# Loading an image by colour channel, another order of the last attention turn, and one transpose for half a group's maxima

## The reference

```python
# tokenizer: 8 images of 256 x 256 x 3, then 128 text rows of width 256 each
g = einsum('bhwc,cd->bhwd', x, ccm) + ccm_bias
g = sum(slopes * relu(g[..., None] - shifts), axis=-1)      # 16 points, slopes are 0 beyond the first
h = clip(einsum('bhwc,co->bhwo', g, conv_w) + conv_b, 0, 1)[..., 0]
h = concatenate([h, txt], axis=1)                           # 8 x 384 tokens of width 256
# causal attention, 16 heads of 16, keys and values through a latent of 64
c_kv = ln(h) @ W_DKV;  k = c_kv @ W_UK;  v = c_kv @ W_UV;  q = ln(h) @ W_UQ
h = h + softmax(causal(q @ k.T / 4)) @ v @ W_O
# 8 experts, the two best per token, 384 slots per expert and choice
scores = softmax(ln(h) @ router_w)
y_e = gelu(x_e @ w1[e]) @ w2[e]                             # 256 -> 1024 -> 256
h = h + sum over the two choices of y * weight + bias
```

## Time and profile before

| | |
|---|---|
| median of three runs | 658.73 us (657.36 to 666.75) |
| the profiled execution | 664.39 us, span 662.7 us |
| PE, PEld busy | 608.2 us (92%), 508.2 us |
| DVE, ACT, POOL busy | 399.6, 377.1, 388.4 us |
| share of the last chain | PE 80%, ACT 5%, issue 5%, DVE 3% |
| front half, expert half | about 0 to 366 us, 366 to 663 us |

### The profile page before, as it was taken

The page is one execution under the profiler, slowest core; times in us unless marked ns, Lnnn a source line. Parts: engine busy times, 40 slices in busy tenths (PEclk is TensorE's granted clock), DMA queues, the critical chain, the costliest instruction groups (busy, mean ns, idle before and its releaser), DMA issues.

```text
span 662.7 us, 13744 instructions
## 1 busy us (share of the span) xinstructions
PE 608.2 (92%) x5082; PEld 508.2 (77%) x5082; DVE 399.6 (60%) x950; ACT 377.1 (57%) x818; POOL 388.4 (59%) x602
## 2 busy tenths in 40 slices
PE   1788999999999999999878899999999999999992
PEld 1465666676767666666558899999999999999992
DVE  5789788788998888678464333334554555344320
ACT  4448786777777785765641554445454454545540
POOL 4303233424556555556556499998877777888223
PEclk9979999999999999999899799999999999999997
DMA  6437676633534232371012825454444434442113
GB/s 231 124 80 179 196 203 179 182 102 99 145 98 113 72 104 82 105 221 36 34 48 63 285 93 110 115 112 112 112 110 81 97 82 105 112 109 45 20 23 38
DMA packets 66604, 73.86 MB, mean 111 GB/s; under 512 B 6312, under 2 KB 61586, under 8 KB 66536
## 3 DMA queue, kind: packets, MB, share of 16 engines
q1 hardware_dynamic: 56232, 59.45, 30.3%
q0 software_dynamic: 9504, 13.00, 11.5%
q10 hardware_dynamic: 800, 0.52, 0.3%
HBM read 31.62 MB, written 22.48 MB: 82 GB/s over the span
## 4 chain that ended last, share of the span: by engine, by line
PE 80%; ACT 5%; issue 5%; DVE 3%; DMA 2%; SPq 1%; POOL 1%; ACTq 0%; DVEq 0%; POOLq 0%
PE t_bank L1790 20%; PE bank L1805 14%; PE s_bank L1805 7%; PE bank L695 7%; PE t_bank L660 5%; PE s_bank L638 5%; PE t_bank L754 3%; PE s_bank L639 2%; PE t_bank L723 2%; PE s_bank L1775 1%; PE t_bank L738 1%; PE t_bank L760 1%; PE bank L707 1%; DVE g L1235 1%; ACT part L1032 1%
## 5 line engine op out<-in xcount | busy, mean ns | idle before, releaser
L1752 DVE TENSOR_TENSOR hl<-h,hh 128x384 fp32r<-128x384 f32 x128 | 102.9, 809 | 157.9 <-ACT h L1715 157.9
L553 POOL TENSOR_SCALAR_AFFINE_SELECT pt<-pt 128x256 f32<-128x256 f32 x192 | 82.0, 433 | 150.2 <-ACT pt L973 116.7
L1192 DVE TENSOR_REDUCE mx<-s_bank 128x2 f32<-128x256 f32 (+2 forms) x192 | 122.9, 683 | 34.2 <-PE s_bank L639 33.7
L1712 ACT ACTIVATE hh<-t_bank 128x384 fp32r<-128x384 f32 x128 | 63.0, 492 | 135.0 <-PE t_bank L1790 132.7
L1665 POOL DMA_INDIRECT out<-yo,xr x48 | 74.8, 1558 | 59.1 <-ACT yo L1723 48.9
L973 ACT ACTIVATE pt<-t_bank 128x512 f32<-128x512 f32 x128 | 76.1, 602 | 30.6 <-PE t_bank L660 29.4
L1652 POOL TENSOR_TENSOR wl<-wr,wh 128x256 fp32r<-128x256 f32 x112 | 92.5, 859 | 1.2
L1790 PE MATMUL t_bank<-xh,wh 128*128 128x384 f32 x256 | 87.1, 340 | 0.6 <-DVE xl L1746 0.6
L1790 PE MATMUL t_bank<-xl,wh 128*128 128x384 f32 x256 | 86.5, 338 | 0.0
L1790 PE MATMUL t_bank<-xh,wl 128*128 128x384 f32 x256 | 86.4, 338 | 0.0
L638 PE MATMUL s_bank<-ks,qs 96*128 96x128 bf16 (+2 forms) x384 | 80.0, 278 | 1.6 <-DMA ks<-part 1.5
(11 more groups left out here) (205 smaller groups left out, 1341.4 us busy)
## 6 DMA issues: line engine op xcount, KB each, us to landing
wr<-in_w SPq DMA_DIRECT2D x16, 1024.0 KB, 5.8
qs<-part SPq DMA_DIRECT2D x96, 96.0 KB
ks<-part SPq DMA_DIRECT2D x90, 96.0 KB
slot_rows<-empty SPq DMA_DIRECT2D x4, 1560.0 KB, 9.4
xr<-slot_rows SPq DMA_DIRECT2D x16, 390.0 KB, 3.3
wr<-in_x SPq DMA_DIRECT2D x8, 768.0 KB, 5.5
out<-hid SPq DMA_DIRECT2D x8, 384.0 KB, 6.2
qs<-mT ACTq DMA_DIRECT2D x64, 3.0 KB
```

The source lines that it names most:

```text
L553: pool.affine_select(out=blocks, in_=blocks, compare_op=ALU.is_ge, fill=0.0, base=0, pattern=[[0, 2], [1, P]], channel_multiplier=-1).then ...
L1192: ins = dve.tensor_reduce(mx[:, p // 2, j, 2 * (p % 2):2 * (p % 2) + 2], pair_region(s_bank, j), AX_X, ALU.max)
L1752: dve.tensor_tensor(hl[:, f, :], h[f % 2][:, :], hh[:, f, :].bitcast(F32), ALU.subtract).then_inc(hl_done, 1)
```

## The change

Seven groups of edits are made together.

- Image 0 comes in three transfers, one for each colour channel, with a semaphore each; ACT waits for the first alone, DVE for the second and the third.
- On POOL the clearing of `empty`, the `token` table and the ones of `vb` move behind the first root; the split of `up` leaves POOL: its high part goes to ACT, its low part to DVE, between the variances and the scaling of entry 0. The statistics of entry 0's text rows move on DVE ahead of its colours.
- The maxima are kept heads before tiles, so one transpose of 128 x 24 takes the place of three of 128 x 8; ACT copies 24 x 128 in place of 8 x 384, and each of the two rows goes out from 12 partitions of 256 bytes in place of 4 of 768. In the last turn SP issues these two transfers for heads 4 to 7, not ACT.
- The last turn is reordered: PE ranks entry 5 earlier, projects entry 6 later and transposes entry 6's rows after projecting entry 7; ACT copies turn 14's contexts after the last exponentials; DVE makes entry 5's slots first, splits the first expert's first matrix itself (copy and subtraction, two halves) between its attention work, and POOL sends entry 5's rows between its clips.
- PE's fillers become full-precision (f32) ones: `turned` (128 columns each) in seven places and `spinning` (11 of 512 columns) in place of the last 200.
- The bias of the last entries moves on DVE into the first expert unit, and SP loads the second expert's weights ahead of the stores.
- POOL's one subtraction of 2048 columns becomes eight of 256.

```diff
-        load_x(0)
+        wide = IT * W
+        for c in range(CH):
+            sp.dma_start(xin[0][:, c, :, :].rearrange("p j w -> p (j w)"),
+                         x[0][:, c * wide:(c + 1) * wide]).then_inc(x_first[c] if c < CH - 1 else x_in[0], 16)
...
-        pool.memset(empty[:, :, :], 0.0).then_inc(empty_made, 1)
...
-        pool.wait_ge(mats_in, 16)
-        pool.tensor_copy(up_h[:, :], up).then_inc(up_split, 1)
-        pool.wait_ge(up_split, 1)
-        pool.tensor_tensor(up_l[:, :], up, up_h[:, :].bitcast(F32), ALU.subtract).then_inc(up_split, 1)
         rstds(0)
+        pool.wait_ge(xn_done, NT)
+        pool.memset(empty[:, :, :], 0.0).then_inc(empty_made, 1)
...
         for p in range(4):
             for unit in range(3):
                 clip(END, p, unit)
+            if p:
+                send(B - 3, p - 1)
         rstds2(B - 2)
-        for i in range(TOPK * NT):
-            send(B - 3, i)
+        send(B - 3, 3)
+        pool.wait_ge(cx_sb, NG * END + 2)
+        send(B - 3, 4)
         rstds2(B - 1)
+        send(B - 3, 5)
...
-            for j in range(NT):
-                mm = pe.transpose(M_b[0:MPARTS * GH, j * P:(j + 1) * P],
-                                  ms[:, grp, j, :, :].rearrange("p a h -> p (a h)"), ident_b[:, :])
-            mm.then_inc(mT_ps, 1)
+            pe.transpose(M_b[0:MPARTS * GH * NT, 0:P], ms[:, grp, :, :, :].rearrange("p a h j -> p (a h j)"),
+                         ident_b[:, :]).then_inc(mT_ps, 1)
...
+        def turned(count):
+
+            for _ in range(count):
+                pe.matmul(t_bank[:, 1, 0:P], ident[:, :], ident[:, :], start=True, stop=True)
+
+        def spinning(count):
+
+            pe.wait_ge(empty_made, 3)
+            flat = empty.rearrange("p k d -> p (k d)")
+            for _ in range(count):
+                pe.matmul(t_bank[:, 1, :], ident[:, :], flat[:, 0:512], start=True, stop=True)
...
-            act.activation(mT[:, grp, :], M_b[0:MPARTS * GH, 0:T], ACT.Copy).then_inc(mT_sb, 1)
+            act.activation(mT[:, grp, :], M_b[0:MPARTS * GH * NT, 0:P], ACT.Copy).then_inc(mT_sb, 1)
...
+        text_norms(0)
         for i in range(6):
             colours(0, i)
...
+        dve.wait_ge(up_split, 1)
+        dve.tensor_tensor(up_l[:, :], up, up_h[:, :].bitcast(F32), ALU.subtract).then_inc(up_split, 1)
         scaled(0)
...
-        early_low(dve)
-        for b in range(LATE, B):
-            late_bias(b)
...
-        stores(sp)
         for i in range(2):
             load_weights(1, i)
+        stores(sp)
...
+    def early_first(dve, half):
+
+        cols = slice(half * NW // 2, (half + 1) * NW // 2)
+        dve.wait_ge(w_in[0], 16)
+        dve.tensor_copy(wh[0][0][:, cols], wr[0][:, cols]).then_inc(w_first[0], 1)
+        dve.wait_ge(w_first[0], half + 1)
+        dve.tensor_tensor(wl[0][0][:, cols], wr[0][:, cols], wh[0][0][:, cols].bitcast(F32),
+                          ALU.subtract).then_inc(w_split[0], 1)
```

More of the change, by code:

```diff
@@ L139, in _ @@
         def _(dve):
-            before.vector(dve, behind.early_low)
-            behind.vector(dve)
+            before.vector(dve, behind.early_first)
+            behind.vector(dve, before.biases)
 def front(nc, common, lent, wr, w_in, routed, x, txt, params, mats, w1, w2, slot_rows, out):
@@ L273, in front @@
     x_in = [sem(f"x_in{q}") for q in range(2)]
+    x_first = [sem(f"x_first{c}") for c in range(CH - 1)]
     empty_made = sem("empty_made")
@@ L412, in store, with max_rows @@
                      hid[:, b, :, :]).then_inc(res_out, 16)
+    def max_rows(queue, n, grp):
+        queue.wait_ge(mT_sb, NG * n + grp + 1)
+        for a in range(MPARTS):
+            queue.dma_start(qs[(n // 2) % 2][n % 2][MROW + a:MROW + a + 1, grp * GH:(grp + 1) * GH, :],
+                          mT[a * GH * NT:(a + 1) * GH * NT, grp, :]).then_inc(m_in[grp], 16)
     def stores(sp):
@@ L774, in rows_back @@
             if b == B - 2:
-                take("last" if c else "logits", rowT_sb, KC * b + c + 1)
+                take("ranks" if c else "logits", rowT_sb, KC * b + c + 1)
             else:
@@ L923, in tensor @@
         shifted_scores(END, 0, 2)
+        ranks(B - 3)
         shifted_scores(END, 1, 0)
@@ L928, in tensor @@
         contexts_back(END - 1, 1, False)
-        project(B - 2, 0)
-        ranks(B - 3)
         shifted_scores(END, 2, 0)
@@ L939, in tensor @@
         shifted_scores(END, 3, 1)
+        project(B - 2, 0)
         shifted_scores(END, 3, 2)
+        project(B - 2, 1)
         values(END, 1)
+        turned(2)
         contexts_back(END, 1, False)
+        turned(3)
+        contexts_out(END, 0)
+        turned(2)
+        for k in range(2):
+            project(B - 1, k)
         for c in range(KC):
             rows_back(B - 2, c)
-        contexts_out(END, 0)
-        for k in range(2):
-            project(B - 1, k)
+        turned(3)
         router(B - 2)
-        turning(30)
+        turned(7)
         for c in range(KC):
@@ L1056, in scalar @@
         act.activation(uq, uq, ACT.Copy, scale=float(SCALE)).then_inc(prepared, 1)
+        act.activation(up_h[:, :], up, ACT.Copy).then_inc(up_split, 1)
         for d in range(CH):
@@ L1177, in scalar, with late_bias, vector @@
         gates(B - 1)
-    def vector(dve, early_low):
+    def late_bias(dve, b):
+        dve.wait_ge(row_done, (NT + 1) * b + NT + 1)
+        dve.tensor_tensor(hid[:, b, :, :], hid[:, b, :, :],
+                          bias.rearrange("p (o d) -> p o d", o=1).to_broadcast([P, NT, DIM]),
+                          ALU.add).then_inc(res_last, 1)
+    def vector(dve, early_first):
         steps = [0]
@@ L1230, in colours @@
             c, d = 1 + i // CH, i % CH
+            if b == 0 and d == 0:
+                dve.wait_ge(x_first[1] if c == 1 else x_in[0], 16)
             if c == 1:
@@ L1492, in vector @@
         mark(B - 3)
+        weigh(B - 3)
+        keep_ranks(B - 3)
+        place(B - 3)
         reciprocals(END - 1, 1)
         normalise(END - 1, 1)
+        dve.wait_ge(t_ready, 12 * END)
+        early_first(dve, 0)
+        reciprocals(END, 0)
+        normalise(END, 0)
+        early_first(dve, 1)
         residual(B - 2, 0)
         norms2(B - 2, (0, 1))
-        weigh(B - 3)
-        reciprocals(END, 0)
-        normalise(END, 0)
         residual(B - 2, 1)
@@ L1502, in vector @@
         variances2(B - 2)
[L1503 to L1505 removed]
         reciprocals(END, 1)
         normalise(END, 1)
+        scaled2(B - 2)
         residual(B - 1, 0)
@@ L1686, in early_high @@
     def early_high(act):
-        for i in range(2):
-            act.wait_ge(w_in[i], 16)
-            for half in range(2):
-                cols = slice(half * NW // 2, (half + 1) * NW // 2)
-                act.activation(wh[i][0][:, cols], wr[i][:, cols], ACT.Copy).then_inc(w_first[i], 1)
-    def early_low(dve):
+        act.wait_ge(w_in[1], 16)
         for half in range(2):
             cols = slice(half * NW // 2, (half + 1) * NW // 2)
-            dve.wait_ge(w_first[0], half + 1)
-            dve.tensor_tensor(wl[0][0][:, cols], wr[0][:, cols], wh[0][0][:, cols].bitcast(F32),
-                              ALU.subtract).then_inc(w_split[0], 1)
+            act.activation(wh[1][0][:, cols], wr[1][:, cols], ACT.Copy).then_inc(w_first[1], 1)
+    def early_first(dve, half):
[5 more added lines that the diff above has]
+                          ALU.subtract).then_inc(w_split[0], 1)
     def scalar(act):
@@ L1763, in vector @@
                     hidden(u + 1, f)
+                if u == 0 and f in BIAS_AT:
+                    biases(dve, BIAS_AT.index(f))
                 if u + 2 < U and f == ROWS_AT:
```

85 lines of the change are left out of this document (40 added, 45 removed).

## The result

The changed kernel takes 655.5 us, the median of 20 runs (652.77 to 657.84), where the kernel before takes 659.79 us in 20 runs (657.09 to 666.75). The ratio is 0.9925, with an interval of [0.9903, 0.9948]: 5.0 us less, between 3.4 and 6.4 (the two medians alone lie 4.3 us apart). That is within 2%. It is 3.1 us short of the 8.1 us foreseen; the time itself lies 4.9 us above the forecast of 650.6 us and only 0.5 us inside the end of the range, 656.0 us. The profiled execution took 655.22 us with a span of 653.5 us, at its median; that of before lay 4.6 us above the median of its 20 runs.

What follows compares the result with a forecast made beforehand. PE was taken to bound the kernel, with gains only at the start, in its attention instructions and before the experts. 2.4 + 2.8 + 2.9 = 8.1 us off 658.73 gave 650.6 us, range 644.0 to 656.0.

Steps and rivals of the forecast that it cites:

- the maxima: Attention turns: two fewer PE transposes, 32 times, save 3.5 us of PE; taken as 2.8 us, between 0 and 3.5.
- the turn with the sends: Last turn to the experts' first rows: 1.0 us from reordering plus 1.9 from sends, 2.9 us, between 0.9 and 4.2.
- the clock at the experts' start is full: Experts' start: a listed sign that the prediction is wrong, since it expected the half-clock stretch there to stay.
- Start: Kernel start: earlier parameters and first channel 1.4 us, shorter colour instruction 1.0; 2.4 us, between 1.0 and 3.2.
- The long colour instruction: DVE at the start: the last colour instruction should take about 0.74 us instead of 1.76, winning 1.0 us.
- three transfers would land no earlier: Image load at the start: parameters land as before; 1.4 us less gain, 652.0 us, within a rival of chance 0.18.
- In the PE-bound middle this is time: Attention turns: step counting PE's saved transposes as run time, except where DVE ends the wait; four fifths taken, 2.8 us.
- The rival that I had priced, the rows landing late: Maxima transfers: 12 short pieces make PE wait each half group; 666.6 us at 0.5 us each; chance 0.05.
- The sends: POOL's three first-choice sends of entry 7: DVE's subtractions and bias no longer beside them; 1.9 us won.
- first rival: Last ranks and experts' start: the clock stays up, 2.2 us plus 1.4 us more gained, 647.0 us; chance 0.18.
- the 0.7 us given back: Last turn: entry 6's rows, f32 fillers and router 6's delays take 0.7 us from the 1.7 us won.
- I leave the clock as it was: Experts' start: PE's gap before the first rows stays over 3 us, so no clock gain was counted.

Runs made afterwards that it cites:

- e1: The kernel before with the start edits alone (image 0 by channel, POOL's and DVE's order, split of `up`): 663.34 us, ratio 0.9973 to the kernel before.
- e2: The kernel before with the maxima edits alone (one transpose per half group, short copy, 12-piece transfers): 667.32 us, ratio 1.0025 to the kernel before.
- e5: The whole change with the old maxima (three transposes, rows in 4 pieces of 768 bytes): 652.83 us, ratio 0.9893 to the kernel before.
- e7: The whole change with one transfer of 24 pieces per half group's maxima instead of two of 12: 653.57 us, ratio 0.9900 to the kernel before.
- e11: The change with the old maxima, but one transfer of 8 pieces of 768 bytes per half group: 652.53 us, ratio 0.9884 to the kernel before.
- e9: The whole change with 170 bf16 products of 128 columns replacing the last filler of 11 f32 products: 658.04 us, ratio 0.9948 to the kernel before.
- e10: The whole change with the three bias additions on DVE directly behind the last ranks again: 656.51 us, ratio 0.9942 to the kernel before.
- e12: The whole change run once more with no edit: 655.2 us, ratio 0.9921 to the kernel before.
- e4: The whole change with the old bf16 fillers in their old places: 667.21 us, ratio 1.0014 to the kernel before.
- e3: The whole change without its start and maxima parts: 657.64 us, ratio 0.9886 to the kernel before.
- e6: The kernel before with only its three fillers behind the last turn replaced by the new f32 ones: 660.73 us, ratio 1.0006 to the kernel before.
- e8: The change with the old maxima plus six f32 filler products on PE in turn 0: 652.66 us, ratio 0.9894 to the kernel before.

## Why the prediction was right in its range and 3.1 us off

The time came into the range by luck. One of the three terms of the sum, the maxima, had the wrong sign; another, the turn with the sends, was foreseen at less than half of what its part gives alone; and the clock at the experts' start is full, which the prediction itself had named as a sign that it is wrong.

**Start: right, somewhat small.** Foreseen 2.4 us. PE's first transposes come at 17.93 us and not 19.95, 2.0 us earlier; alone the part gives 1.8 us (e1). The long colour instruction went as foreseen. The parameters came 0.93 us earlier and not 1.4, and DVE waited 0.96 us for the text, whose statistics I had only moved. The Trainium skill ("DMA: Bandwidth & Descriptors", Rules for kernel authors) wants many small transfers made into one, and the prediction read from it that three transfers would land no earlier. The pieces here are 256 KB, and the trace shows a gain. (The upper bound of 3.2 us is not in the working: 1.7, 1.0 and 0.4 make 3.1.)

**Maxima: the step that failed.** Foreseen 2.8 us gained; alone 1.7 us lost (e2), and the change without it is 2.1 us faster by the ratios (e5 against the change). The step that failed is "In the PE-bound middle this is time". In the table the seven kernels with the old maxima take 212.24 to 212.91 us from the 5th to the 28th, the seven with the new 213.09 to 214.87, though PE has some 2.5 us less to do there (23 times 0.11). Three things happened.

First, a saving on PE lasts only to PE's next wait. PE is busy 97% of the middle, and I read that as "PE ends every wait"; but the rest is waits on ACT and DVE in every turn, and their chains did not get shorter. The longest waits of PE from 70 to 300 us, in e5 and in the change:

```profile
PE t_bank L763 <- DVE ckvT L1414: 2.3, 6, 0.4
PE t_bank L669 <- ACT pt L999: 0.4, 1, 0.4
PE bank L677 <- DVE ms L1235: 0.3, 1, 0.3
PE bank L716 <- ACT cx L1013: 0.3, 1, 0.3
```

```profile
PE t_bank L761 <- DVE ckvT L1412: 2.3, 6, 0.4
PE t_bank L761 <- ACT part L1053: 1.4, 6, 0.2
PE t_bank L738 <- DVE hid L1254: 1.1, 3, 0.4
PE t_bank L669 <- ACT pt L997: 0.5, 1, 0.5
PE t_bank L764 <- ACT part L1053: 0.3, 1, 0.3
```

The six waits for `part` of up to 0.2 us are new: PE is there sooner and waits. Over the first 8 half groups of the stretch only 0.10 us of 0.88 is left, and behind them nothing of the saving shows: from one transpose to the next, e5 and the repetition of the change agree within 0.03 us, but for three places.

Second, the new layout made DVE's two small instructions for `ms` slower where POOL works beside them. Their line in the kernel before and in the change:

```profile
L1201 DVE CAST ms<-mx x32: 166/166/167, 41.1 to 318.2; 128x12 bf16<-128x12 f32 x32
```

```profile
L1229 DVE CAST ms<-mx x32: 172/173/420, 38.9 to 318.1; 128x12 bf16<-128x12 f32 x32
```

And DVE, POOL and PE at one such place of the change:

```profile
174.23 0.33 DVE L1229 CAST ms<-mx 128x12 bf16<-128x12 f32 x1
174.48 0.22 DVE L1239 RECIPROCAL rs<-bank 128x12 f32<-128x12 f32 x1
174.62 0.30 DVE L1233 TENSOR_TENSOR ms<-mx,ms 128x12 bf16<-128x12 f32 x1
```

```profile
174.11 0.78 POOL L555 TENSOR_SCALAR_AFFINE_SELECT pt<-pt 128x256 f32<-128x256 f32 x2
```

```profile
176.98 0.52 PE L738 MATMUL t_bank<-ident,xn 128*128 128x128 f32 x3 [0.37 <-DVE hid L1254]
```

In e5 the same two take 0.17 and 0.15 us, beside the same clip. Three such places (174, 212 and 250 us) make the three waits of up to 0.4 us for `hid`: 1.1 us. They are the three places just named: there the step from one transpose to the next is 0.3 to 0.4 us longer in all seven kernels with the new maxima than in all seven with the old. Three times 0.33 less the 0.10 us won is the 0.9 us that lies between e5 (212.27) and the repetition (213.14). The Trainium skill ("SBUF — State Buffer", Who interferes with whom) says that a copy or cast on DVE may use a second port pair that it shares with GpSimd, and that one of the two then blocks. The rows agree with it: the cast that writes three separate runs of four values never varies, the one that writes 12 adjacent values is longer beside POOL. That the layout is the cause is read from 14 profiles and was not tried by itself; the usual length of the issues on ACT's queue, 0.72 us for 0.58, was tried and is not it (e7, e11).

Third, single issues on that queue were slow. The middle is 0.9 to 1.8 us longer still in e2, e9 and the first profile of the change than in e7, e10 and e12. In these three the two issues near 264 us (266 in e2) take 2.65 to 3.06 us. The change and its repetition:

```profile
263.94 2.76 ACTq L418 DMA_DIRECT2D qs<-mT  x2
```

```profile
264.29 1.54 ACTq L418 DMA_DIRECT2D qs<-mT  x2
```

ACT's next copy starts 2.87 us behind the first issue and not 1.65, and the step between the two transposes around it is 0.8 to 1.2 us longer in the three profiles. In e2 and e9 two issues near 102 us take 2.2 us for 1.6, and that step is 0.5 us longer. No profile with the old maxima has an issue of over 1.26 us; why a few take up to 2.3 us is open. What is left are casts of 0.35 to 0.40 us in other places, two in e2 and three in e4 (213.60 us), each with a step 0.2 us longer. The rival that I had priced, the rows landing late, did not come: `qs<-mT` was waited for 0.4 us in all, 0.5 before.

**Turn and sends: the terms named were there, their sum was too small.** Foreseen 2.9 us; alone 7.6 us (e3, between 5.7 and 9.6). The sends are right: 1.87 us against 1.9. The last `values` comes 2.75 us earlier, 1.3 us of which are a half-clock stretch at 320 us of the profile before (the same steps took 1.25 us less in e1, in the old order at full clock); the last `ranked` on DVE starts 4.03 us earlier, with the 1.36 us of the earlier trace rows in it. Third, the send's landing took 1.6 us less, which is chance: in e2 and e6, with the old order's sends, it took as little as in the change, and in e9 nearly as much as before. Fourth, that wait of 1.36 us goes with the old fillers. The clock falls to 0.50 at the last ranks in all four profiles that have 30 and 20 bf16 products ahead of them (before, e1, e2, e4), and in one of the ten with f32 ones (e10). The prediction had this only in its first rival. (e3 waited 0.88 us there at full clock, so the clock need not be all of it.) Last, the old filler: in the new order it holds PE to 369.3 us (e4), so the new order needs the new filler for its gain; I had asked only what the new one would hold. The new fillers ahead of the last ranks cost nothing, since PE still waits 0.51 us for DVE behind them; I had them in the 0.7 us given back.

**Clock: "I leave the clock as it was" was wrong for this profile, and could not be read from one.** I had reasoned that the wait for the first rows stays over 3 us; it is 0.98 us. With full clock at their start the experts take 293.0 to 293.1 us (four profiles), with a half-clock stretch 294.5 to 295.7 (ten): 1.4 to 2.6 us, around the first rival's 2.2. But a wait of 1 us does not decide it: e5 and e8 have the same fillers there and waits of 1.06 and 1.08 us, and the clock fell in e8's profile only; it fell in e7's too, after 0.95 us. Over the 29 runs of the kernel before on the first chip, 0.01 of mean granted clock goes with 3.7 us; there e3 has 0.9885 in the median and before 0.979. By this estimate 3.5 of its 7.6 us go with the clock.

**The sum.** The parts alone give 1.8 - 1.7 + 7.6 = 7.7 us, the whole 5.0, with an uncertainty of about 3 us on the sum of three. Most of that gap lies between the start and the turn: together they give 7.1 us (e5), not 9.4; whether it is more than noise is open. Mending the second term alone, 2.4 - 1.7 + 2.9 = 3.6 us gives 655.1. So the forecast was near by two errors of opposite sign, which is luck: 4.5 us too much on the maxima, 4.7 us too little on the turn. Subtracting from the median was right: of the 4.6 us by which before's profile lies above it, 2.9 are the fall of the clock at 320 us (1.3 us) and the slow landing (1.6 us), both absent in e2, of the same order. The fall at 348 us is no part of it, since e1 and e2 have it too; the other 1.7 us are open.

## What to carry to other kernels

An engine that is busy 97% still hands each saving to the next wait, so count a saving on it only up to there. Ahead of an event that moves earlier, look for fillers: one that fitted the old wait holds the work in the new one, and here 11 long instructions did better than 200 short ones. When POOL works beside a small DVE instruction on a busy chain, look at the longest and not only the median duration of its line before you change its layout.

## What the runs showed of the chip

- A row of short PE instructions can run dry: 200 bf16 products of 128 columns broke up after 104 (e4) and 187 (e1) into groups of one to six, mostly 1.43 us from group to group, while rows were sent and loaded; 170 did not break in one profile, in which the load began 1.5 us before their end. What it waits for is not in the profile.
- An issue on ACT's queue took 0.58 us for 4 pieces, 0.62 for 8 or 24 and 0.72 for 12 in the median, and this difference did not reach the time. Single issues of 1.9 to 2.3 us, in three of the profiles with 12 pieces, held ACT and went with a loss of 0.8 to 1.2 us.
- DVE's instructions over two SBUF inputs stretched POOL's sends from 0.97 us: beside the bias to 1.39 and 1.43 (e10), in the kernel before to 1.65 beside f32 subtractions of 128 x 1024 and to 1.70 and 1.43 beside the bias.
- Where the clock falls in the first 66 us changes from one execution to the next of nearly the same program, and of the same one: the change had 0.50 in 58 to 60 us in one profile and 1.00 in another. With the new start the fifth transpose of maxima came at 72.86 to 76.44 us.
